# One-hot bytes of the second merge: made in both edge stages instead of the first alone

## What is computed

```
def conv(x, src, dst, edge_attr, W_msg, W_edge, W_root, b):
    msg = x[src] @ W_msg + edge_attr @ W_edge
    agg = segment_max(msg, dst, num_segments=N)
    agg = where(isneginf(agg), 0.0, agg)
    return agg + x @ W_root + b
c1 = leaky_relu(conv(X,  src, dst, edge_attr, W1_msg, W1_edge, W1_root, b1))
c2 = leaky_relu(conv(c1, src, dst, edge_attr, W2_msg, W2_edge, W2_root, b2))
return layernorm(x + c2)
```

## Time and profile before

| | us |
|---|---|
| median of 3 runs | 1858.12 |
| lowest, highest | 1848.87, 1861.15 |
| profiled execution | 1853.45 |
| its span in the trace | 1851.7 |

### The profile page before, as it was taken

One profiled execution on the slowest core, in us unless ns is written; L12 is line 12 of the kernel. 1 busy time (PEld: TensorE's weight loads), 2 busy tenths in 40 slices (PEclk: granted clock), 3 DMA queues, 4 the chain that ended last, 5 costly groups with the idle time before them and its releaser, 6 DMA issues.

```text
span 1851.7 us, 36622 instructions
## 1 busy us (share of the span) xinstructions
PE 1535.6 (83%) x11422; PEld 1370.8 (74%) x11422; DVE 1280.4 (69%) x1945; ACT 1066.1 (58%) x2402; POOL 995.5 (54%) x1454
## 2 busy tenths in 40 slices
PE   3998888888899999986898989988988776666764
PEld 2677777777779888885787778877878776665664
DVE  3677767766776665554677667776737888888777
ACT  2354555444453555653555555555537888888887
POOL 6777777777610000003777777777747555454443
PEclk9999999999999999997999999999999888798877
DMA  7779999899874788885788887888868999999997
GB/s 147 205 198 265 272 265 268 266 272 271 255 251 160 235 265 277 288 287 185 201 236 235 224 229 226 243 226 241 229 211 244 297 297 291 298 301 299 274 275 210
DMA packets 505019, 459.10 MB, mean 248 GB/s; under 512 B 348553, under 2 KB 412340, under 8 KB 504836
## 3 DMA queue, kind: packets, MB, share of 16 engines
q1 hardware_dynamic: 444118, 321.15, 61.9%
q0 software_dynamic: 30976, 57.72, 12.9%
q10 hardware_dynamic: 29742, 77.88, 10.7%
HBM read 283.25 MB, written 173.37 MB: 247 GB/s over the span
## 4 chain that ended last, share of the span: by engine, by line
PE 32%; DMA 26%; POOL 15%; DVE 11%; issue 8%; ACT 6%; SPq 1%; ACTq 0%; DVEq 0%; POOLq 0%
PE ps L590 20%; POOL arena_hold L416 13%; DMA onehot_bytes<-arena_hold 13%; DMA arena_hold<-in_x_dram 6%; PE ps L501 4%; DVE arena_hold L927 4%; DMA arena_hold<-nodes,src_perm 4%; ACT arena_hold L769 3%; PE ps L492 2%; PE ps L469 2%; DMA out_dram<-arena_hold 2%; POOL onehot L449 2%; PE ps L462 2%; DVE arena_hold L913 1%; ACT arena_hold L715 1%
## 5 line engine op out<-in xcount | busy, mean ns | idle before, releaser
L590 PE MATMUL ps<-arena_hold,onehot 128*128 x4688 | 617.2, 295 | 161.9 <-POOL onehot L449 131.0
L590 PEld LDWEIGHTS ps<-arena_hold,onehot 128*128 128x128 f32 x4688 | 591.2, 208 | 188.1 <-issue 186.0
L416 POOL DMA_INDIRECT arena_hold<-nodes,src_perm x392 | 370.0, 944 | 458.4 <-SPq L383 339.2
L501 PEld LDWEIGHTS ps<-w_root,onehot 97*128 97x128 f32 x3136 | 408.7, 197 | 102.3 <-issue 101.8
L416 POOL DMA_INDIRECT arena_hold<-in_x_dram,src_all x392 | 375.0, 957 | 141.6 <-issue 113.8
L501 PE MATMUL ps<-w_root,onehot 97*128 97x128 f32 x3136 | 425.0, 280 | 0.0
L654 ACT COPY arena_hold<-ps 128x384 f32<-128x384 f32 x392 | 187.9, 479 | 285.2 <-PE ps L501 283.9
L449 POOL CAST onehot<-keep 128x256 f32<-128x256 uint8 x588 | 208.8, 406 | 201.9 <-ACT ps L693 140.0
L913 DVE TENSOR_TENSOR_SCAN arena_hold<-keep,arena_hold,ps 96x512 f32<-96x512 bf16 x196 | 247.7, 1264 | 47.2 <-PE ps L469 46.6
L927 DVE TENSOR_TENSOR onehot<-count,rel 128x1024 f32<-128x1024 bf16 x147 | 179.5, 1222 | 126.4 <-PE ps L590 124.9
L927 DVE TENSOR_TENSOR arena_hold<-ps,rel 128x1024 uint8<-128x1024 f32 x147 | 175.2, 1216 | 109.1 <-DMA onehot_bytes<-arena_hold 108.5
(11 more groups left out here) (97 smaller groups left out, 1207.5 us busy)
## 6 DMA issues: line engine op xcount, KB each, us to landing
root<-arena_hold ACTq DMA_DIRECT2D x196, 384.0 KB
arena_hold<-root SPq DMA_DIRECT2D x196, 384.0 KB, 4.1
nodes<-arena_hold SPq DMA_DIRECT2D x98, 384.0 KB, 3.0
arena_hold<-nodes SPq DMA_DIRECT2D x98, 384.0 KB
arena_hold<-in_x_dram SPq DMA_DIRECT2D x97, 384.0 KB
arena_hold<-in_x_dram SPq DMA_DIRECT2D x48, 768.0 KB, 9.1
out_dram<-arena_hold SPq DMA_DIRECT2D x48, 768.0 KB, 6.6
onehot_bytes<-arena_hold SPq DMA_DIRECT2D x147, 128.0 KB
```

Source lines behind the costliest of these rows:

```text
L416: nc.gpsimd.indirect_dma_start(out=gathered[t.ring][0:t.p, i, 0:D], out_offset=None, in_=table_in, in_offset=bass.IndirectOffsetOnAxis(ap= ...
L501: last = nc.tensor.matmul(no_ps[m % 2][:, i * P:(i + 1) * P], nodes_t[m % NODE_RING][0:D + 1, i * P:(i + 1) * P], w_root[0:D + 1, layer * ...
L590: nc.tensor.matmul(ps_bytes[:, bass.ds(place_at, SLOT)].bitcast(F32), onehot[:, k % NS, i, :], rows_from(t)[:, bass.ds(word, SLOT)].bitcas ...
```

## The change

Batches 0 to 72 are made in groups 15 to 97 of edge stage 0 as before, but spread over the same groups, so that a group has one at most. Batches 73 to 146 are made in groups 2 to 89 of edge stage 1, behind the second leaky maximum of the nodes. The counts are copied into PSUM once in each edge stage (merge 0 writes over them), and TensorE waits for that copy. SyncE stores the bytes in both stages. The wait for all stores moves from ahead of edge stage 1 to behind it on SyncE, and POOL gets one ahead of its first load of bytes.

```diff
+BYTES_ON = 2
+BYTES_OFF = 8
+    NBATCH_0 = NBATCH // 2
-        def byte_batches(g):
-            span = NE - BYTES_AT
-            return range((g - BYTES_AT) * NBATCH // span, (g + 1 - BYTES_AT) * NBATCH // span) if g >= BYTES_AT else range(0)
+        def byte_batches(layer, g):
+            first, after = (BYTES_AT, NE) if layer == 0 else (BYTES_ON, NE - BYTES_OFF)
+            done, more = (0, NBATCH_0) if layer == 0 else (NBATCH_0, NBATCH - NBATCH_0)
+            span = after - first
+            return range(done + (g - first) * more // span, done + (g + 1 - first) * more // span) if first <= g < after else range(0)
...
 (SyncE, edge_phase)
-                    if layer == 0:
-                        for k in byte_batches(g - EDGE_RING):
-                            store_bytes(k)
+                    for k in byte_batches(layer, g - EDGE_RING):
+                        store_bytes(k)
...
 (SyncE, between the stages)
+            sp.sem_inc(ready, 1)
+            edge_phase(1)
             for i in range(2):
                 sp.wait_ge(bytes_stored[i], DMA * ((NBATCH + 1 - i) // 2))
-            sp.sem_inc(ready, 1)
-            edge_phase(1)
...
 (POOL, behind the gathers of layer 1)
+            for i in range(2):
+                pool.wait_ge(bytes_stored[i], DMA * ((NBATCH + 1 - i) // 2))
...
 (TensorE, turn_back)
-                if t.layer == 0 and t.g >= BYTES_AT:
-                    pe.wait_ge(bytes_made, byte_batches(t.g).stop)
+                if t.g == (BYTES_AT, BYTES_ON)[t.layer]:
+                    pe.wait_ge(count_set, t.layer + 1)
+                if byte_batches(t.layer, t.g):
+                    pe.wait_ge(bytes_made, byte_batches(t.layer, t.g).stop)
...
 (VectorE, edge_phase)
-                        if g == BYTES_AT:
-                            then(nc.vector.tensor_copy(count_ps, count[:]))
-                        for k in byte_batches(g):
-                            make_bytes(k)
+                    if g == (BYTES_AT, BYTES_ON)[layer]:
+                        nc.vector.tensor_copy(count_ps, count[:]).then_inc(count_set, 1)
+                        dve.wait_ge(count_set, layer + 1)
+                    for k in byte_batches(layer, g):
+                        make_bytes(k)
```

More of the change, by code:

```diff
@@ L199, in gnn @@
         no_full, root_read, root_stored = sem("no_full"), sem("root_read"), sems("root_stored", UNIT_RING)
-        primed, made, bytes_made, grown, opened = (sem(n) for n in ("primed", "made", "bytes_made", "grown", "opened"))
+        primed, made, count_set, bytes_made, grown, opened = (sem(n) for n in ("primed", "made", "count_set", "bytes_made", "grown", "opened"))
         bytes_stored, bytes_in = sems("bytes_stored"), sems("bytes_in")
@@ L315, in edge_phase @@
                         load_nodes(layer, u)
-                    if layer == 0:
-                        for k in byte_batches(g - EDGE_RING):
-                            store_bytes(k)
+                    for k in byte_batches(layer, g - EDGE_RING):
+                        store_bytes(k)
                 for u in unit_loads.get((layer, NE), ()):
                     load_nodes(layer, u)
-                if layer == 0:
-                    for g in range(NE - EDGE_RING, NE):
-                        for k in byte_batches(g):
-                            store_bytes(k)
+                for g in range(NE - EDGE_RING, NE):
+                    for k in byte_batches(layer, g):
+                        store_bytes(k)
             def load_root(layer, u):
```

## The result

The changed kernel takes 1829.91 us (median of 4 runs, 1828.09 to 1830.15) against 1855.38 us before (4 runs): a ratio of 0.9867, 95% interval 0.9842 to 0.9891. The profiled execution has a span of 1828.0 us, 23.7 less than the 1851.7 of before.

The account below looks back on a forecast made before the run. Store waits held POOL back in edge stage 0; POOL's gather issue was stage 1's floor. 23.2 us gained minus 0.5 gave 22.7: 1830.5 against the profiled execution, 1835 against the median, forecast 1834, range 1822 to 1852.

Parts of the forecast that it names:

- POOL's delay in stage 0: Edge stage 0: the 15.7 us by which POOL's gathers are held back goes; last gather at about 502.6 instead of 518.3.
- the list at its end: Expected profile signs: stage 0 store and compare waits near 0, POOL's a few us; stage 1 as long to 1 us.
- The engines come closer to POOL: End of edge stage 0: last scan 13.8 us behind the last gather instead of 21.3, another 7.5 us gained.
- The compares in stage 1: Edge stage 1, VectorE: 74 added compares fit its idle time, mean 4.70 us a group under POOL's 5.00; cost 0.5 us.
- SyncE's queue: Edge stage 1: 74 stores each wait about 2.4 us for their compare, ahead of the next loads; cost 0.
- DMA traffic: Edge stage 1: stores add about 22 GB/s, to near 250, without gathers landing too late; cost 0.
- the 8.7 us of room: Edge stage 1: some 8.7 us between a buffer's last gather landing and POOL being held by it.
- The rule of the Trainium skill: Edge stage 1: DMA engines alternate queues by packet, so stores put off gathers; at most 0.57 us, sum 22.1 not 22.7.
- Rival 1: Edge stage 0: store wait goes but engines stay some 20 us behind POOL; gain 8 to 16 us; chance 0.22.
- the two terms: Edge stage 0: POOL's 15.7 us delay and the engines' 7.5 us catching up, together 23.2 us.
- Rival 2: Edge stage 1: compare lengthens a group to 5.51 us, outgrowing POOL; 28 us lost, 1863 us in all; chance 0.10.
- Rival 3: Edge stage 1: a running compare stops POOL's gathers, losing up to 90 us, 1925 in all; chance 0.03.

Follow-up runs that it names:

- e1: Kernel before the change, all 147 batches still in edge stage 0, but three byte buffers instead of two: 1826.30 us, ratio 0.9855.
- e5: Changed kernel without the compares and stores of edge stage 1, merge 1 loading first-half batches again: 1824.67 us, against 1826.19 for the changed kernel on the same chip.
- e7: Changed kernel with each batch of edge stage 1 stored four times, three of them into spare tensors: 1826.21 us, ratio 0.9872.
- e2: Changed kernel with all 147 batches made in edge stage 1 and none in stage 0: 1854.51 us, ratio 1.0011.
- e6: Changed kernel with 110 batches in edge stage 0 (1.33 a group) and 37 in stage 1: 1825.49 us, ratio 0.9871.

## Why the prediction was right

- *POOL's delay in stage 0.* Forecast: last gather at 502.6, 15.7 us earlier. Measured 503.9, 14.4 earlier. The compare's wait, the transpose back's wait and POOL's wait went as the list at its end said, and L467 waits 33.8 us for rows.
- *The engines come closer to POOL.* Forecast 13.8 us behind the last gather, 7.5 less than before. Measured 514.24 - 503.87 = 10.4 us, 10.9 less. This term was too small by 3.4 us. The 13.8 was read from one profile's stage 1: in the profile of after the last scan of stage 1 comes 10.6 us behind the last gather, in e1 12.6. Where a late landing falls may decide it; that was not followed. The last scan of stage 0 moved by 25.3 instead of 23.2.
- *The compares in stage 1.* Forecast 0.5 us; e5 and the change differ by 0.4, which can't be told from nothing, since stage 1 without compares takes 498.6 to 502.1 us in three profiles and 499.4 and 499.0 in two of the changed kernel. That they are hidden is shown, the 0.5 is not. VectorE's period with a compare was forecast at 4.78 and is 4.56, because its operations start closer together than they last: the compare takes 1.21, and the next operation starts 1.13 behind it. The estimate of the mean, 4.70, was further off, since a group without a compare can take 3.43 rather than 4.29; it is about 4.4. Either is under 5.00, so the sum didn't change. VectorE's idle time before the edge maximum fell from 118.9 us to 53.5 (860 to 1330 us, a window as long as that of the earlier trace rows), where some 40 were forecast.
- *SyncE's queue.* I had a wait of 2.4 us for each compare; it is 97.4 us in 73 places, 1.3 each (860 to 1330 us), and the wait for the scan fell from 319.0 to 196.1. No wait of TensorE or VectorE for SyncE's loads is in the lists of stage 1.
- *DMA traffic.* Forecast 0, near 250 GB/s; measured 253, and no loss. With four stores a batch (e7) the gathers still take 488.2 us, and TensorE's wait for them is 46.2 us against 41.9 and 45.1: the 8.7 us of room were not used up. The rule of the Trainium skill (DMA: Bandwidth & Descriptors, Queues, rings and completion order) would have made the sum 22.1 instead of 22.7; 0.6 us is too little to be seen here, and with four times the stores these runs show no loss by it.
- *Rival 1* (stage 0 gains in part) did not come: the two terms together gave 25.3 us where 23.2 were forecast. *Rival 2* did not come with one compare a group; with 1.67 the stage does outgrow POOL (e2), because VectorE's own work is too much. *Rival 3* is excluded: POOL's gathers of stage 1 last 946 ns in the median and 962 at most beside 74 compares, and their pitch is that of before.

Against the profiled execution the sum was 22.7 us, and the spans differ by 23.7. Stage 0 gave 25.3 (the engines' term 3.4 more, POOL's 1.3 less than forecast). From its last scan to the first gather of stage 1 it is 320.1 us against 318.8, which took back 1.3. Stage 1 gave 2.7 (499.4 us against 502.1 from the first gather to the last scan, most of it because the last scan comes 10.6 instead of 13.8 us behind the last gather; my list had the stage as long as before to 1 us), and merge 1 took back 3.0. The last three were forecast at nothing or at 0.5 and nearly cancel, so that the sum comes within 1 us of the spans is in part luck. What is borne out is stage 0's two terms and that stage 1 costs nothing.

The medians differ by 25.5, because the profiled execution of before lies 1.9 us below the median of its four runs and that of after at its own. The forecast of 1834 had added most of the 4.7 us by which the median of three runs stood above the profiled one. On the chip of e5 the gain is 24.7 us (1850.89 - 1826.19).

## What to carry to other kernels

When a stage is slower than its slowest engine's instructions explain, look for a wait on a small ring of buffers before looking at the work: here a third buffer gave what the moved work gave. A long wait is no price by itself: 60.8 us of it cost nothing (e6), since POOL was not held. Work added to an engine off the limit was free here while the engine's own period stayed under the limiting engine's, and that period is to be read from start to start in back-to-back rows, with light and heavy groups averaged: one compare a group fitted under POOL's 5.00 us, 1.67 did not. Once the wait was gone the limit was the gather's issue, and further shifts of the compares gave nothing.

## What the runs showed of the hardware

The DMA share of a window did not say how much more the engines could carry: at 0.89 they moved 253 GB/s, at 1.00 they moved 319 (e7), and the gathers kept their pitch.

Some of POOL's gathers in stage 0 last up to 1.88 us instead of 0.95. Of 15 that last over 1.05 us, 14 lie beside operations with which VectorE builds the tables of the merge and the indices of stage 1, from SBUF to SBUF. POOL's and VectorE's timelines of the changed kernel:

```profile
52.79 1.88 POOL L419 DMA_INDIRECT arena_hold<-in_x_dram,src_all  x1 [0.30 <-issue]
...
52.40 1.45 DVE L847 SCALAR_TENSOR_TENSOR arena_hold<-arena_hold 128x1176 f32<-128x1176 f32 x1
...
56.77 1.88 POOL L419 DMA_INDIRECT arena_hold<-in_x_dram,src_all  x1 [0.30 <-issue]
...
56.38 1.44 DVE L847 SCALAR_TENSOR_TENSOR arena_hold<-arena_hold 128x1176 f32<-128x1176 f32 x1
```

Beside a compare, whose counts come from PSUM, gathers take 0.94 and 0.95 us. The Trainium skill (SBUF — State Buffer, Who interferes with whom) has a pair of ports that VectorE and GpSimd share, and counts operations with at most one input from SBUF, outside the modes with two ports, as free of it. The rows agree in kind; no run here moved the table operations, so that they are the cause is not shown. The longer gathers add some 6 us to POOL's 498 in stage 0.
